# Sinkhorn in three chains of 5, 8 and 3 sequences inside the autocorrelation, and mixing by blocks of small diagonals

## What is computed

```
H_res = sinkhorn_log(x_norm @ W_res.T + base)      # 4 x 4 per token, 50 iterations, tau 0.1
H_res = (1 - g) * I + g * H_res
x_mixed[t, i] = sum_j H_res[t, i, j] * x[t, j]     # streams of 256 channels
y = (sum_j H_pre[t, j] * x[t, j]) @ W_branch
out[t, i] = x_mixed[t, i] + y[t] * H_post[t, i]
```

## Time and profile before

| What | Value |
|---|---|
| time, median of 3 runs | 1298.62 us (1297.89 to 1299.15) |
| time of the profiled execution | 1296.82 us |
| its span, first to last instruction | 1295.0 us |
| PE busy | 1070.1 us, 83% |
| DVE busy | 989.8 us, 76% |
| ACT busy | 616.4 us, 48% |
| POOL busy | 546.5 us, 42% |

### The profile page before, as it was taken

One profiled execution on the slowest core, in us unless ns is written; L12 is line 12 of the kernel. 1 busy time (PEld: TensorE's weight loads), 2 busy tenths in 40 slices (PEclk: granted clock), 3 DMA queues, 4 the chain that ended last, 5 costly groups with the idle time before them and its releaser, 6 DMA issues. The chain is left out here.

```text
span 1295.0 us, 24193 instructions
## 1 busy us (share of the span) xinstructions
PE 1070.1 (83%) x8048; PEld 826.3 (64%) x8048; DVE 989.8 (76%) x2908; ACT 616.4 (48%) x1758; POOL 546.5 (42%) x678
## 2 busy tenths in 40 slices
PE   5699999999999999996479999998788874096182
PEld 4477777777877777775356677776566543085071
DVE  6766677766666677765158777787999898999998
ACT  6444455555444455555156776776455542311110
POOL 2523344333333444333137665665454340153194
PEclk9799999999999999998789999999998885597596
DMA  8011101111111101111222232232122111622012
GB/s 362 23 56 40 54 18 55 55 55 55 55 53 41 48 23 55 56 40 40 100 87 76 87 122 85 75 117 86 65 75 70 37 57 41 245 74 89 16 66 97
DMA packets 28652, 95.43 MB, mean 74 GB/s; under 512 B 3760, under 2 KB 7856, under 8 KB 28592
## 3 DMA queue, kind: packets, MB, share of 16 engines
q1 hardware_dynamic: 28592, 94.69, 20.0%
HBM read 64.27 MB, written 27.26 MB: 71 GB/s over the span
## 5 line engine op out<-in xcount | busy, mean ns | idle before, releaser
L614 POOL TENSOR_TENSOR prob_G<-prob_G,rl 128x512 f32<-128x512 f32 x96 | 100.0, 1042 | 258.1 <-DVE rl L502 258.1
L384 ACT ACTIVATE prob_G<-prob_G,negm 128x128 f32<-128x128 f32 x384 | 148.8, 388 | 89.6 <-DVE negm L444 89.6
L245 PE MATMUL ps_qkv<-w_hi,xT_hi 128*128 128x512 f32 x384 | 156.2, 407 | 13.5 <-DVE prob_G L507 8.5
L246 PE MATMUL ps_qkv<-w_lo,xT_hi 128*128 128x512 f32 x384 | 151.4, 394 | 0.0
L247 PE MATMUL ps_qkv<-w_hi,xT_lo 128*128 128x512 f32 x384 | 150.9, 393 | 0.0
L317 PE MATMUL ps_qkv<-wo_hi,aT_hi 128*128 128x512 f32 x256 | 108.0, 422 | 0.0
L319 PE MATMUL ps_qkv<-wo_hi,aT_lo 128*128 128x512 f32 x256 | 102.3, 399 | 0.0
L318 PE MATMUL ps_qkv<-wo_lo,aT_hi 128*128 128x512 f32 x256 | 102.1, 399 | 0.0
L245 PEld LDWEIGHTS ps_qkv<-w_hi,xT_hi 128*128 128x128 f32 x384 | 73.0, 190 | 39.4 <-issue 16.5
L1482 PE MATMUL p_out<-m_xr,m_diag 128*128 128x256 f32 x240 | 58.1, 409 | 46.9 <-POOL m_diag L1649 37.0
L440 DVE TENSOR_TENSOR prob_G<-ps_s,mask 128x512 f32<-128x512 f32 x96 | 65.0, 677 | 41.6 <-PE ps_s L228 41.1
(11 more groups left out here) (218 smaller groups left out, 2987.7 us busy)
## 6 DMA issues: line engine op xcount, KB each, us to landing
rows<-c_row SPq DMA_DIRECT2D x16, 640.0 KB, 3.3
xin<-in_x SPq DMA_DIRECT2D x16, 512.0 KB, 3.3
xres<-in_x SPq DMA_DIRECT2D x16, 512.0 KB, 5.3
x<-xres SPq DMA_DIRECT2D x16, 512.0 KB, 2.6
c_xin<-x SPq DMA_DIRECT2D x16, 512.0 KB, 5.0
c_cin<-in_ctx SPq DMA_DIRECT2D x16, 512.0 KB, 4.3
c_b_xres<-x SPq DMA_DIRECT2D x16, 512.0 KB, 3.2
m_late_row<-rows SPq DMA_DIRECT2D x10, 640.0 KB, 10.9
```

The costliest lines, as they stand in the source:

```text
L245: nc.tensor.matmul(ps_qkv[:, n, :], xT_hi[:, k, :], w_hi[:, k, cols], start=k == 0, stop=False)
L246: nc.tensor.matmul(ps_qkv[:, n, :], xT_hi[:, k, :], w_lo[:, k, cols], start=False, stop=False)
L384: r = nc.scalar.activation(prob(g)[:, j, :], prob(g)[:, j, :], ACT.Exp, bias=negm[:, h:h + 1], accum_out=lsum[:, h:h + 1])
L614: nc.gpsimd.tensor_tensor(prob(g), prob(g), rl[:, g * GROUP:(g + 1) * GROUP].rearrange("p (j o) -> p j o", o=1).to_broadcast([P, GROUP, T] ...
```

## The change

Sequences are split into chains `a` (0 to 4), `b` (5 to 12) and `c` (13 to 15). All three are begun in the autocorrelation, and `steps_to` and `logs_at` say by hand how far each has come by every part of every body. `beside` is also called after each `tq` product, after each of the four products at L1204 and after each weighting at L1275. `weave` issues steps of two chains in turn. At the end of the phase `a` has all 308 steps, `b` 126 and `c` 16. Bodies 5 and 6 are now written out (`LOOPED = 4`).

```diff
-RESTART = 13
-EARLY_LEFT = 3
-EARLY = 6
+ROWS_OF_CHAINS = (5, 8, 3)
+LOOPED = 4
...
+def weave(dve, *targets):
+    while any(chain.issued < to for chain, to in targets):
+        for chain, to in targets:
+            advance(dve, chain, to, 1)
...
-        shares = {EARLY + 1: (2, 0, 1, 0, 3), EARLY + 2: (0, 0, 1, 0, 1),
-                  **{b: (0, 0, 14, 0, 16) if b == EARLY + 3 else (5, 8, 12, 0, 5) for b in range(EARLY + 3, RESTART)},
-                  RESTART: (3, 8, 20, 2, 5)}
-        shares.update({b: (5, 8, 12, 0, 5) for b in range(RESTART + 1, B - 1)})
-        shares.update({B - 1: (8, 0, 14, 0, 20), B: (8, 0, 8, 0, 20), B + 1: (1000, 0, 0, 0, 0)})
...
+        steps_to = {(6, 0): ((one_a, 2),), (6, 2): ((one_a, 3),), (6, 4): ((one_a, 6),),
+                    (7, 1): ((one_a, 7),), (7, 2): ((one_a, 8),)}
+        at = 8
+        for b in range(8, B - 1):
+            if b == 11:
+                parts = {0: at + 3, 1: at + 9, 2: END[0], 3: END[1], 4: END[1] + 10}
+            else:
+                parts = {0: at + 3, 1: at + 9, 2: at + 29, 4: at + 40}
...
+        steps_to[14, 0] += ((one_b, 2),)
+        steps_to[14, 2] += ((one_b, 3),)
+        steps_to[14, 4] += ((one_b, 6),)
+        steps_to.update({(15, 0): ((one_b, 8), (one_a, END[2])), (15, 1): ((one_b, 22),), (15, 2): ((one_a, END[3]), (one_b, 46)), (15, 3): ((one_b, 50),),
+                         (15, 4): ((one_b, 56),), (16, 0): ((one_b, 88),), (16, 3): ((one_c, 2),), (16, 4): ((one_b, 100), (one_c, 6)),
+                         (17, 0): ((one_b, 116),), (17, 4): ((one_b, 126), (one_c, 16))})
+        logs_at = {(6, 1): ((one_a, 1),), (6, 2): ((one_a, 2),), (7, 0): ((one_a, 3),), (7, 1): ((one_a, 4),), (7, 2): ((one_a, 5),),
+                   (11, 2): ((one_a, 6), (one_a, 7), (one_a, 8)),
+                   (14, 1): ((one_b, 1),), (14, 2): ((one_b, 2),), (15, 0): ((one_b, 3), (one_b, 4), (one_b, 5)),
+                   (15, 1): ((one_a, 9), (one_a, 10)), (15, 2): ((one_a, 11),),
+                   (16, 2): ((one_c, 1), (one_c, 2)), (17, 2): ((one_c, 3), (one_c, 4), (one_c, 5))}
...
                         nc.vector.tensor_tensor(dst[:], src, of[:], ALU.mult).then_inc(tw_done, 1)
+                        beside(b, 2)
```

```diff
-                    sp.dma_start(rows[b - 2], row[par][:]).then_inc(row_out[par], 16)
+                    for g in range(NS):
+                        lanes = slice(g * W, (g + 1) * W)
+                        sp.dma_start(rows_x[b - 2].rearrange("(j t) g c -> g t j c", j=NS)[g],
+                                     row[par][lanes, 0:D].rearrange("p (j c) -> p j c", j=NS)).then_inc(row_out[par], 16)
+                    sp.dma_start(rows_y[b - 2], row[par][:, D:ROW]).then_inc(row_out[par], 16)
```

```diff
+                    for g in range(NS):
+                        if 0 < n <= LAST:
+                            pe.wait_ge(out_done, NS * (n - 1) + g + 1)
...
+                        nc.tensor.matmul(p_out[:, g, 0:C], d[:, g * NS:(g + 1) * NS, :].rearrange("p i t -> p (i t)"),
+                                         xm[n][:, g, :], start=True, stop=False)
+                    for g in range(NS):
+                        lanes = slice(g * W, (g + 1) * W)
+                        nc.tensor.matmul(p_out[:, g, 0:C], d[lanes, N2:N2 + NS, :].rearrange("p i t -> p (i t)"),
+                                         ym[n][lanes, :], start=False, stop=True).then_inc(mix_ps, 1)
...
+            copies(one_a)
+            take_out(0, 2)
+            logs(one_b, FIRST_LOGS + 1, FIRST_LOGS + BLOCK_LOGS)
+            take_out(2, one_a.n)
+            logs(one_c, FIRST_LOGS + 1, FIRST_LOGS + BLOCK_LOGS)
+            logs(one_b, FIRST_LOGS + BLOCK_LOGS + 1, FIRST_LOGS + 2 * BLOCK_LOGS)
+            copies(one_b)
+            take_out(one_b.first_row, LAST - 1)
+            logs(one_c, FIRST_LOGS + BLOCK_LOGS + 1, FIRST_LOGS + 2 * BLOCK_LOGS)
+            take_out(LAST - 1, LAST)
+            copies(one_c)
+            take_out(LAST, B)
```

More of the change, by code:

```diff
@@ L741, in sinkhorn_step, with advance, autocorrelation_phase @@
     return chain.iteration((k - BASES[n] - 2) % 6 + 1)
[L744 removed]
+def advance(dve, chain, to, most=1000):
+    for k in range(chain.issued + 1, min(to, chain.issued + most) + 1):
+        if k > 1:
+            dve.wait_ge(chain.step, k - 1)
+        if k in (3, 4, 7, 8):
+            dve.wait_ge(chain.logs, {3: 1, 4: 2, 7: 3, 8: 4}[k])
+        for n in range(len(BLOCK_ITERS)):
+            if k == BASES[n] + 2:
+                dve.wait_ge(chain.logs, FIRST_LOGS + n * BLOCK_LOGS)
+            if k == BASES[n + 1] - 1:
+                dve.wait_ge(chain.logs, FIRST_LOGS + n * BLOCK_LOGS + 2)
+        sinkhorn_step(chain, k).then_inc(chain.step, 1)
+        chain.issued = k
+def weave(dve, *targets):
+    while any(chain.issued < to for chain, to in targets):
+        for chain, to in targets:
+            advance(dve, chain, to, 1)
+def autocorrelation_phase(nc, x1, ctx_in, ident, dft, w24, base, wb, norm2, facts, chains, rows_x, rows_y):
     with ExitStack() as ctx:
@@ L849, in autocorrelation_phase @@
[L849 to L860, removed]
@@ L1355, in _, with mixing_phase @@
             iterations(pool, body)
-def mixing_phase(nc, rows, facts, early, gate, ident, out):
+def mixing_phase(nc, rows_x, rows_y, facts, chains, gate, sel, fold, out):
     with ExitStack() as ctx:
@@ new lines, in take_out @@
+            def take_out(first, to):
+                for n in range(first, to):
+                    chain = max((c for c in chains if c.first_row <= n), key=lambda c: c.first_row)
+                    spread_ready(act, chain)
+                    for g in range(NS if n < LAST else 2):
+                        act.wait_ge(mix_ps, NS * n + g + 1)
+                        nc.scalar.activation(ot[n][:, g, :], p_out[:, g, 0:C], ACT.Identity,
+                                             bias=mean[:, n, g:g + 1]).then_inc(out_done, 1)
@@ L1544, in both @@
-            def both(k, compute):
-                for chain in chains:
-                    if not isinstance(k, int) or k > 1:
-                        dve.wait_ge(chain.step, k - 1)
-                    compute(chain).then_inc(chain.step, 1)
-            def logs_done(k):
-                for chain in chains:
-                    dve.wait_ge(chain.logs, k)
-            issued = [BASES[2] - 2 - 6 * EARLY_LEFT]
-            def early_iterations(steps):
-                for k in range(issued[0] + 1, min(issued[0] + steps, BASES[2] - 2) + 1):
-                    dve.wait_ge(early.step, k - 1)
-                    sinkhorn_step(early, k).then_inc(early.step, 1)
-                    issued[0] = k
```

472 lines of the change are left out of this document (200 added, 272 removed).

## The result

The changed kernel takes 1278.47 us (median of 4 runs, 1277.55 to 1278.83), beside 1298.88 us (1297.89 to 1300.64) for the kernel before in the same job. The ratio is 0.984, with a 95% interval of 0.9823 to 0.9857: 1.6% faster. Forecast were 1271 us and a range of 1250 to 1290, so the sign and the range held, and the time is 7.5 us above the forecast. The profiled execution took 1278.3 us, its span 1276.4.

What follows compares the result with a forecast made beforehand. DVE was taken to bound the kernel from 887 us to the end. 1296.8 + 33.8 (dearer autocorrelation) - 61.1 (shorter mixing phase) = 1269.5 us profiled; the median, 1.8 above, 1271 us; range 1250 to 1290.

Steps and rivals of the forecast that it cites:

- Bodies 13 to 15: Autocorrelation: body 13 -0.5 us, body 14 +2, body 15 +8.5 before its products and +3.2 after them.
- A sequence on TensorE at 2.9 us: Mixing phase: 1.73 us of stream records, the 32-lane records four at once, and 0.55 for the copy out.
- One sequence at 1.2 GHz a block: Mixing phase: PE begins at the lower clock after idling, so a first sequence takes about 5 us, not 2.9.
- just hidden: Mixing phase: seven sequences of b are copied out by 110 us, beside c, which reaches its logarithms at 111.
- `c`'s stalls with GpSimd: Mixing phase: POOL's eight blocks of 1.3 us stall c's 103 remaining steps by 4 us.
- The stall of 8 us: Mixing phase: DVE, ready at 14.1 us, waits for b's logarithms at 22.3, behind ACT's copies of sequences 0 and 1.
- The first (more hidden): Whole kernel: woven steps cost 0.2 us, b's stall is short; autocorrelation +22, mixing 125, 1250 us; chance 0.15.
- The second, TensorE as the bound: Mixing phase: PE stays at 1.2 GHz or 32-lane matmuls run singly; 13 to 25 us more, 1283 to 1295; chance 0.15.
- the small price that I took: Mixing phase on PE: changing tiling mode costs 0.1 us at either edge of a sequence's 32-lane part.
- The third: Autocorrelation: steps between the four products hold back POOL's sums, PE's output and next body; 1357 us, slower; chance 0.06.
- The fourth: Mixing phase: c's steps are the real length, 292 at 0.355, 104 us plus tail; no chance of its own.
- The signs on record: Bodies from the eighth at 30 to 32 us, L1627 gone, PE mixing records 400 to 256, c alone 1.5 us an iteration.

Runs made afterwards that it cites:

- the reordering: Changed kernel, but in the autocorrelation ScalarE takes a chain's first-block logarithms after its copies of key spectrum and transposed weights; 1271.8 us, ratio 0.980.
- The idle matmuls: Changed kernel plus idle matmuls into a bank of their own around each block of mixing, to keep TensorE busy; 1270.2 us, ratio 0.979.
- six banks: Changed kernel with the mixing output p_out rotating over six PSUM banks where it used four; 1272.4 us, ratio 0.980.
- the 28 steps of body 15: Changed kernel with 28 of chain b's steps taken out of body 15 and put off into the mixing phase; 1271.1 us, ratio 0.979.
- the run without steps in the products: Changed kernel with the chain steps after each of a body's four products issued alone at the end of that part; 1279.4 us, ratio 0.985.
- the four edits: Changed kernel with b's logarithms before copies, autocorrelation copies before logarithms, six PSUM banks and idle matmuls into the next bank; 1261.8 us, ratio 0.972.

## Why the prediction was right, and where it was off

Its sum for the profiled execution was 1269.5 us; that took 1278.3, so 8.8 us are missing. The median stood 0.2 us above the profiled execution, not 1.8, which leaves 7.2, or 7.5 against the rounded 1271.

**The autocorrelation: forecast +33.8, measured +36.9.** From the intervals of the stores:
- Up to the chain: -1.1 for 0. Bodies 6 and 7 (to row 6): +3.6 for +1. The sum had the logarithms at 1 us and left out what is queued behind them on ScalarE; the reordering gave some 2.3 us back.
- Body 8 (to row 7): +9.0 for +7.5. Bodies 9 to 12 (to row 11): +5.2 for +7. Together as forecast, and so was the price inside them: `a`'s 47 multiplications of each kind average 588 ns from 866 to 1082 us (the groups of VectorE), for 0.24 undisturbed, which is 2 x 47 x 0.35 / 7 = 4.7 us a body, forecast 2.9 + 1 to 2.
- Bodies 13 to 15 (to row 14): +15.0 for +13.2. `a`'s last two multiplications of logarithms took 0.99 and 2.12 us, and VectorE idled 1.72 and 1.02 us for `b`'s. The sum had steps and one table load there. This is read from the trace; no run was made for it.
- Bodies 16 and 17, to the end of the phase: +5.3 for +5.1.

The copies of 1 KB pieces and SyncE's five stores cost nothing, as forecast: a body without steps still takes 23.21 us (746.90 to 770.11).

**The mixing phase: forecast 134, measured 139.7.** From its start (1136.7 us):

| | forecast | measured |
|---|---|---|
| rows of a on hand | 10.7 | 12.9 |
| DVE ready for b's logarithms | 14.1 | 16.0 |
| its idle time there | 8 | 10.5 |
| b's logarithms | 22.3 | 26.0 |
| b's last logarithms | 79 | 80.2 |
| b's coefficients | 80.5 | 83.0 |
| c at its logarithms | 111 | 114.7 |
| b's copies out | 110 | 116.4 |
| c's last logarithms | 111 | 117.7 |
| end | 134 | 139.7 |

The terms that failed are two. *A sequence on TensorE at 2.9 us*: it was 3.31. The stream part took 1.97 for 1.73, the part with 32 lanes 0.71 for 0.65, the wait for the copy 0.62 for 0.55. *One sequence at 1.2 GHz a block*: there were two at the start of `a` and of `b`. Up to the seventh copy of `b` that is 6 x 0.4 + 1.8 = 4.2 us; with 2.5 us from `b`'s later coefficients it makes 6.7, against the 6.4 by which these copies were late. So they were not "just hidden": VectorE waited 3.4 us for `c`'s logarithms behind them. The idle matmuls gave back 8.0 us; of the 5.4 us with six banks most goes with the clock of that execution. Two sizes cancelled in part: from `b`'s first to its last logarithms the sum had 56.7 us and 54.2 were measured, though a pair of steps was no cheaper than put (2.17 us for an iteration of both chains, 0.362 a pair), so what was put too high is the waits around them; `c`'s stalls with GpSimd were put at 4 us and measured 6.5.

**The stall of 8 us** was the mechanism that mattered. It was on record with its place and as part of the path; it measured 10.5 us, and removing it shortened the tail by 9.3. What I did not see is that it could be removed by one line of ScalarE's order. I had costed it as part of the phase instead.

**The rivals.** The first (more hidden) fell: the autocorrelation grew by 36.9 us, not 22, and the mixing phase took 139.7, not 125. Only the 28 steps of body 15 were as cheap as it has them, 4.3 / 28 = 0.15 us each. The second, TensorE as the bound, came true in part: it decides at `a` and at the end of `b`, for some 6 us (2.5 and 3.4 us of VectorE's waiting) and not 13 to 25. By the Trainium skill (TensorEngine Tiling (Array Packing), section "Key Properties") two changes of mode a sequence drain the engine; in the run with six banks the sixteen records follow each other in 2.57 us. Eight of the streams take 1.93 of it, 0.24 each; two rounds of four with 32 lanes would be 0.48 and take 0.64, so 0.16 is left for both edges. That is an estimate, which takes four of them to run at once; by it the trace agrees with the small price that I took (0.1 each). The third fell with the run without steps in the products. The fourth had no time of its own. The signs on record came: L1627's groups are gone, TensorE's mixing records went from 400 to 256, the bodies with a full share of steps take 30.3 to 33.3 us, and `c` alone takes 1.52 us an iteration where GpSimd is idle and 2.5 beside one of its blocks.

## What to carry to other kernels

Where a chain of small steps is cut so that its logarithms fall beside other work, look at what stands ahead of them on the engine that takes them: the order there was worth 9 to 10 us here, nearly half of what the whole change brought. Steps put into an idle stretch are free, and cost their price as soon as the stretch is removed, so remove stalls before choosing how much work to move, and don't add up gains measured alone. TensorE, working in short blocks between idle times, ran the first one or two sequences of each at the lower clock; a few idle matmuls ahead of each block were worth 8 us on their own, and did not always suffice.

## What the runs showed that I had not expected

- TensorE needed one or two sequences at 1.2 GHz (0.56 of full clock over 10.8 us) before the clock rose, and how many varied between executions of like kernels, with ends that differ by 2 to 4 us. Block `a` behind 3.9 us of idle matmuls and 3.1 us of idle time ran at 1.00 from its first record. With the four edits as many idle matmuls (4.75 us, then 1.9 us idle) did not bring that: the first sequence took 3.07 us, at 0.59.
- Behind an idle stretch of 7.85 us the selection ran at 1.2 GHz (1.95 us for 1.09). The length of the stretch does not tell it alone: behind 2.17 us the selection ran at 1.00, while behind 2.13 us the fourth sequence ran mostly at 1.2 GHz (granted clock 0.60 over 4.2 us).
- ScalarE loads a table, 1.28 us, at each change between exponential and logarithm seen here: four of them around `b`'s first logarithms in body 15, from 1072.18 to 1079.30 us, for functions of 0.23 to 0.31 us each.
- The autocorrelation of one and the same code differed by up to 4.3 us between executions, in two bodies. What decides it stays open.
